# A cross-attention and FFN kernel: the next block's fourth query product moves from ahead of the seventh values to behind the eighth

## The reference, cut to what matters

```python
x = x + _L0_xattn_ref(_layernorm(x), ctx_1024, ctx_1024, Wq, Wk, Wv, Wo, lam, g)
x = x + _L0_ffn_ref(_layernorm(x), ln1_g, ln1_b, w1, b1, ln2_g, ln2_b, w2, b2)

# _L0_xattn_ref: 16 heads of width 32, 8 key/value heads, two softmax maps for each head
w = softmax(q1 @ k1.T) - lam * softmax(q2 @ k2.T)
attn = w @ v
attn = attn * rsqrt(mean(attn * attn) + EPS) * g * (1.0 - LAMBDA_INIT)
return attn @ Wo.T

# _L0_ffn_ref: both weight matrices are rounded to three levels first
h = gelu(layer_norm(x, ln1_g, ln1_b) @ w1q.T + b1)
out = layer_norm(h, ln2_g, ln2_b) @ w2q.T + b2
```

## Time and profile before

| | |
|---|---|
| median of 3 runs | 2423.88 us (2423.76 to 2427.24) |
| the profiled execution | 2423.49 us, of which the span from first to last instruction is 2421.5 us |
| PE busy | 2286.6 us, 94% |
| DVE busy | 1714.2 us, 71% |
| ACT busy | 1339.7 us, 55% |
| GpSimd busy | 993.4 us, 41% |
| mean granted TensorE clock | 0.983 of full speed |

### The profile page before, as it was taken

How to read it: one execution, slowest core, us unless ns; L and a number is a source line. 1 busy time by engine, 2 the same in 40 slices (tenths; PEclk the granted TensorE clock), 3 DMA queues, 4 the chain that set the end, 5 groups by cost and what they waited for, 6 DMA issues and landing times.

```text
span 2421.5 us, 35774 instructions
## 1 busy us (share of the span) xinstructions
PE 2286.6 (94%) x13791; PEld 1083.1 (45%) x13791; DVE 1714.2 (71%) x2701; ACT 1339.7 (55%) x1945; POOL 993.4 (41%) x807
## 2 busy tenths in 40 slices
PE   8679999999999999999989999999999999999978
PEld 5344534445353544535344454534445453544433
DVE  4677768686785868678676867868676786867663
ACT  3435655556465555656555555655556565555544
POOL 0102625436172534627153452715346271534517
PEclk9779999999999999999999999999999999999989
DMA  7412103030210303021130302112040211203000
GB/s 262 120 25 62 27 24 83 15 92 15 78 30 29 78 15 92 15 66 27 43 79 15 92 15 66 28 47 59 15 107 15 66 28 50 56 15 75 15 22 18
DMA packets 105661, 125.88 MB, mean 52 GB/s; under 512 B 22512, under 2 KB 74284, under 8 KB 104980
## 3 DMA queue, kind: packets, MB, share of 16 engines
q1 hardware_dynamic: 105492, 123.60, 18.4%
HBM read 51.80 MB, written 20.36 MB: 30 GB/s over the span
## 4 chain that ended last, share of the span: by engine, by line
PE 70%; DVE 17%; DMA 3%; ACT 3%; POOL 3%; issue 3%; SPq 1%; POOLq 0%; ACTq 0%; DVEq 0%
PE ps L1421 16%; PE ps L1443 9%; PE ps L1433 9%; PE ps L1319 5%; PE ps L1366 5%; PE ps L1344 4%; PE ps L1264 4%; PE ps L1373 4%; PE ps L1265 3%; PE ps L1266 3%; DVE attn_raw L993 2%; DVE arena L1052 2%; DVE arena L941 2%; DMA arena<-in_x 2%; DVE arena L955 2%
## 5 line engine op out<-in xcount | busy, mean ns | idle before, releaser
L563 POOL TENSOR_TENSOR attn_raw<-attn_raw 128x512 f32<-128x512 f32 x448 | 579.1, 1311 | 153.5 <-ACT attn_raw L720 146.2
L1421 PE MATMUL ps<-rows,w1T 128*128 128x512 f16 x2048 | 486.9, 381 | 24.8 <-DVE rows L1047 24.8
L955 DVE TENSOR_REDUCE arena<-ps 128x3 f32<-128x462 f32 (+1 forms) x704 | 413.0, 618 | 111.0 <-PE ps L1319 110.1
L529 POOL TENSOR_TENSOR q<-q 128x512 f16<-128x512 f32 x128 | 158.3, 1241 | 723.3 <-ACT q L666 706.6
L715 ACT ACTIVATE attn_raw<-ps,vec_cols,wstep 128x512 f32<-128x512 f32 x256 | 198.7, 776 | 276.3 <-PE ps L1421 274.4
L1052 DVE SCALAR_TENSOR_TENSOR arena<-attn_raw,vec_cols,arena 128x512 f16<-128x512 f32 x256 | 231.8, 905 | 86.1 <-ACT arena L718 84.5
L1421 PEld LDWEIGHTS ps<-rows,w1T 128*128 128x128 f16 x2048 | 191.8, 98 | 222.1 <-DVE rows L1047 38.0
L1443 PE MATMUL ps<-w2T,arena 128*128 128x512 f16 x1088 | 271.2, 379 | 0.0
L686 ACT ACTIVATE arena<-ps 128x1024 f32<-128x1024 f32 x128 | 131.6, 1028 | 228.3 <-PE ps L1344 228.3
L975 DVE SCALAR_TENSOR_TENSOR p<-arena,p 128x512 f16<-128x512 f32 x128 | 88.1, 688 | 236.7 <-ACT p L690 236.7
L1319 PE MATMUL ps<-k_att,stack_raw 96*128 96x154 f16 x2048 | 222.0, 233 | 27.2 <-DVE arena L955 25.2
(11 more groups left out here) (183 smaller groups left out, 3478.7 us busy)
## 6 DMA issues: line engine op xcount, KB each, us to landing
stack_raw<-q SPq DMA_DIRECT2D x768, 64.0 KB, 2.0
arena<-in_x SPq DMA_DIRECT2D x64, 256.0 KB, 2.7
out<-arena SPq DMA_DIRECT2D x64, 256.0 KB, 2.1
arena<-in_x SPq DMA_DIRECT2D x15, 1024.0 KB, 6.2
arena<-in_L_ffn_w SPq DMA_DIRECT2D x7, 1024.0 KB, 10.1
stack_raw<-in_L_xattn_Wq SPq DMA_DIRECT2D x8, 256.0 KB, 5.8
k_att<-k_store SPq DMA_DIRECT2D x4, 490.0 KB
k_store<-attn_raw SPq DMA_DIRECT2D x12, 160.0 KB
```

The source lines that it names most:

```text
L563: ins = pool.tensor_tensor(acc[:, e, :], acc[:, e, :], src[:, j % NG, :], ALU.add)
L955: dve.tensor_reduce(negmax[:, tt, u0:u1], ps[:, row_bank(c, tb), 0:(u1 - u0) * S].rearrange("p (u s) -> p u s", s=S), AX.X, ALU.max, negat ...
L1421: ins = pe.matmul(ps[:, B_H + j % 2, :], w1T[:, k, j * P:(j + 1) * P], rows16[:, e, k, :], start=(k == 0 and e == 0), stop=(k == KD - 1 an ...
```

## The change

In the string that blocks 1 to 15 walk, the token `q3` moves from between `s7` and `v6` to between `v7` and `a3`. Block 15 skips it, so the order changes in 14 blocks, 1 to 14. No work is added or taken away.

```diff
 ATTEND = [(w[0], int(w[1:] or 0)) for w in (
-    "e2 g f2 y0 y1 s0 q0 z0 z1 y2 s1 v0 s2 h3 v1 s3 i3 v2 y3 s4 a0 v3 s5 q1 z2 v4 s6 a1 q2 v5 z3 s7 q3 v6 a2 v7 a3").split()]
+    "e2 g f2 y0 y1 s0 q0 z0 z1 y2 s1 v0 s2 h3 v1 s3 i3 v2 y3 s4 a0 v3 s5 q1 z2 v4 s6 a1 q2 v5 z3 s7 v6 a2 v7 q3 a3").split()]
```

## The result

The changed kernel takes 2431.44 us (median of 20 runs, 2427.72 to 2435.14) against 2424.78 before (20 runs, 2420.71 to 2428.84): ratio 1.0026, 95% interval 1.0020 to 1.0033. It is 6.7 us slower; 7.8 was forecast. 2431.7 was predicted, with 2428.6 to 2436.8 as the range. That the time falls 0.3 from the forecast is partly luck: the kernel before, too, measured 0.9 more here than the 2423.88 that the forecast started from.

A forecast was written before the change was run, and what follows sets the result against it. TensorE, busy 94% of the span, and its waits were taken to bound the kernel. 9 x 0.81 + 1.36 - 4 x 0.21 = +7.8 us on the median 2423.88 gave 2431.7, range 2428.6 to 2436.8.

The forecast's parts named there:

- Steps 1 and 2: Behind scores(7), values(6) and values(7) start earlier; the rest of values(7) then stalls on VectorE's L975, as block 15 shows, 1.94.
- Step 3: On VectorE's chain to L975, L997 takes 0.69 instead of 0.90 without L529 beside it: 0.21 off, stall 1.96.
- Step 6: Other engines: the product's ACT operations, L529 beside a reciprocal and SP's later stacking of the pair, costed at nothing.
- Step 4: Behind values(7), TensorE reaches pair 3 and rms_sums 1.36 late: the new stall of 1.96 less the 0.59 wait removed.
- Step 5: At L1007 and hidden, VectorE's slack of 0.55 absorbs part of TensorE's delay, so both come 0.81 late.
- The sum over blocks: Over 14 changed blocks: nine pay 0.81, block 14 pays 1.36, four gain 0.21; +7.8 us.
- The count of four late blocks: In blocks 3, 7, 10 and 11, VectorE's wait for late input rows hides TensorE's delay of 0.81.
- the last sign of being wrong: The forecast is wrong if late transfers fall in blocks other than 3, 7, 10 and 11.
- the 0.21 that each of the four was to gain: In blocks 3, 7, 10 and 11, the input rows' transfer is issued 0.21 earlier, behind L1087.
- The rival "faster": At values(7), L975 is done before 1063.1, so no stall: 11.7 us less, 2412.2; chance 0.05.
- rival on the clock: TensorE falls to 1.2 GHz for the output projection after stalls of 1.96 us; over 70 us, above 2490; chance 0.02.

The follow-up runs named there:

- q3_between: The product q3 put between v6 and v7 (s7 v6 q3 a2 v7 a3), compared with the kernel before: 2422.25 us, ratio 0.9991.
- early_after: Changed kernel with z3 (L1087) and group 7's L975 moved ahead of the reciprocal in normalise(5), compared with the kernel before: 2417.85 us, ratio 0.9972.
- half_before: Kernel before with two of the four row tiles of ln1_rows moved behind h_lo on VectorE: 2410.58 us, ratio 0.9940.
- half_after: Changed kernel with two of the four row tiles of ln1_rows moved behind h_lo, compared with the kernel before: 2420.82 us, ratio 0.9985.
- after_again: The changed kernel run once more, unaltered, compared with the kernel before: 2430.25 us, ratio 1.0027.
- z3_before: Kernel before with z3 (L1087) alone moved ahead of the reciprocal of normalise(5), L975 staying behind: 2415.16 us, ratio 0.9968.
- z3_after: Changed kernel with z3 (L1087) alone moved ahead of the reciprocal of normalise(5), compared with the kernel before: 2426.48 us, ratio 1.0009.
- early_before: Kernel before with z3 (L1087) and group 7's L975 moved ahead of the reciprocal in normalise(5): 2414.31 us, ratio 0.9957.
- early_half_after: Changed kernel with z3 and L975 ahead of the reciprocal and half of ln1_rows behind h_lo, compared with the kernel before: 2401.06 us, ratio 0.9903.
- early_after_late_lo: Changed kernel with z3 and L975 ahead of the reciprocal and L529 behind a3's squares, compared with the kernel before: 2407.45 us, ratio 0.9939.
- all_three: Changed kernel with z3 and L975 early, half of ln1_rows behind h_lo, L529 behind a3's squares, against the kernel before: 2392.34 us, ratio 0.9877.

## Why the prediction was right

- *Steps 1 and 2, a new wait for L975.* Right: the bracket of 1.94, 15 times, 29.0 us with block 15's. Shown by taking it away in two ways: q3_between puts the cover back and the loss goes; early_after brings L975 forward and the stall goes, and with L529 out of the way too the new place is ahead.
- *Step 3, L997 shorter once L529 is elsewhere.* Right: 0.69 in all blocks, and in q3_between too. The Trainium skill's rule (SBUF — State Buffer, Who interferes with whom: VectorE operations with two SBUF inputs and GpSimd's reads exclude each other) also holds for the new place. Step 6 had put L529 beside a reciprocal there, with one input, and it is: L529 starts at 1076.43, the reciprocal lasts from 1075.16 to 1078.51 and keeps its 3.35. What no step priced are the squares of `a2`: they now run beside L1001 and take 1.73 instead of 1.27, without harm: no engine waits for them there. The expectation for early_after left out where L529 would fall, and there the same rule cost 0.8 us a block.
- *Step 4, 1.36 late at `rms_sums`.* Measured 1.34. *Step 5, 0.81 late at L1007 and at `hidden`.* Measured 0.78 and 0.81; half_before against half_after shows the slack to be what takes 1.34 down to 0.8.
- *Step 6, costed at nothing.* L1007 and `hidden` are within 0.03 of where steps 4 and 5 put them, so nothing else reached them.
- *The sum over blocks.* 7.8 by the forecast, 6.7 by the medians with an interval of 4.8 to 8.0, and 8.4 between the two profiled spans. The count of four late blocks held: late rows move `hidden` in blocks 3, 7, 10 and 11 before, in 2, 3, 7 and 11 after, and in 3, 7, 10 and 11 of after_again; those of block 12 after and of block 6 in after_again end within L1007's wait for `rms_sums`, and L1007 keeps its 21.97. But the last sign of being wrong came in part: block 10 was late before, block 2 after. And the 0.21 that each of the four was to gain is lost in how long the transfers take: counted from the undisturbed 35.67, late rows put `hidden` back by 10.9 us in all before, by 11.5 after and by 8.7 in after_again, where 10.9 - 0.8 = 10.1 was forecast. The two traces after lie 1.4 to either side of the forecast, so this term is good on average and not for one trace, and the 1.1 us between forecast and median are no more than it can move. z3_before against z3_after shows what the late rows hide: 11.3 us without them.
- *The rest of 8.4.* At `scores(7)` of block 15 the changed kernel is 9.6 behind (2324.88 against 2315.29) and gets 1.2 back behind it. The profiles differ by such amounts there whatever the change: from that point to the end takes 106.25 before, 105.04 after, and 103.6 to 106.5 in the other runs, all with a granted clock that is for a time at 0.50.
- *The rival "faster"* named the right mechanism with a wrong price. It asked for L975 ahead of the reciprocal and promised 11.7 us under the kernel before. L975 alone does not pay that. With it moved, `values(7)` ends near 7.3 behind `scores(7)`, but VectorE has the reciprocal, L1000 and L1004 to do first, all behind the moved steps, and comes to L988 of `normalise(7)` only at 9.68, no earlier than in the changed kernel (1072.57 - 1062.99 = 9.58); and L992 then hangs on GpSimd. With L529 late, pair 3 comes at 17.78, where the rival had it (1074.57 - 1056.83 = 17.74), but L1007 at 20.63 and not at 20.04, for it ends VectorE's own chain through `ln1_stats`. Against the kernel before with the same VectorE moves, the product's new place costs 3.5 us while L529 falls on L992, and gains 6.9 us once L529 comes later.

That late rows come from the transfers of residual rows and keys issued just ahead is not shown by itself, but the rows speak for it. In block 10 the input rows' load is issued 10.29 behind `scores(7)` before and lands 10.0 us later; in z3_before, where the residual rows are loaded some 4 us earlier, it is issued at 10.22 and lands 5.6 us later. In z3_before and early_before it takes 5.5 to 6.6 us in all of blocks 1 to 13. In early_after it is issued at 7.57, close behind the residual rows again, and takes 8.1 to 9.7 us in blocks 3, 4, 6, 7 and 11; it starts early enough there to be in time all the same. In blocks 3, 7 and 11, z3 also lets it be issued 1.0 us earlier (10.22 instead of 11.25).

## What to carry to other kernels

Work that stands in a place where nobody seems to need it may be the cover of a dependency on another engine: before moving it, look in the trace for what ends last if it goes (here the last block, which lacks the work, showed the 1.94 us stall to be expected). Price a delay at the next point where engines meet, and count how many blocks have slack there for another reason. When an engine's step is moved, check what runs beside it on VectorE and GpSimd in the new place as well as in the old.

## What the runs showed of the hardware

A GpSimd operation on 128x512 held up a VectorE operation with two SBUF inputs that began while it ran: 1.55 us instead of 0.75, and 0.90 instead of 0.69. In q3_between L1001 takes 1.22 instead of 0.69:

```profile
1068.17 1.16 POOL L529 TENSOR_TENSOR q<-q 128x512 f16<-128x512 f32 x1 [7.55 <-ACT q L666]
...
1068.65 1.22 DVE L1001 SCALAR_TENSOR_TENSOR rows<-attn_raw,rows 128x512 f16<-128x512 f32 x1 [0.70 <-ACT rows L694]
```

In each of the three the VectorE operation ends 0.54 to 0.55 us behind GpSimd's. It goes the other way too: in the changed kernel the squares of `a2`, which start 0.08 us behind a VectorE operation with two SBUF inputs (L1001, 0.68 long), take 1.73 us instead of 1.27. In the timelines of VectorE and GpSimd:

```profile
1071.09 0.68 DVE L1001 SCALAR_TENSOR_TENSOR rows<-attn_raw,rows 128x512 f16<-128x512 f32 x1
...
1071.17 1.73 POOL L542 TENSOR_TENSOR sq_acc<-sq_acc,attn_raw 128x512 f32<-128x512 f32 x1 [7.33 <-ACT attn_raw L699]
```

A stall of 1.94 us on TensorE in each of 14 blocks, and one of 3.14, left the granted clock of those stretches at 1.00, the 2.4 GHz level. Other idle times were followed by the 1.2 GHz level, some of them only in some executions. In block 7 of q3_between VectorE waited 5.06 us for input rows and TensorE then idled 4.24; the next matmuls start 0.43 apart instead of 0.22:

```profile
1228.17 0.59 PE L1264 MATMUL ps<-arena,wqT_hi 128*128 128x512 f16 x1 [4.24 <-DVE arena L1016]
...
1229.00:1233.00 4.00, 4.00 (x11) 1.46 (x10) 3.88 (x12) 0.00 (x0) 1.82 (x2) 0.50 0.22 50
```

In block 15 of early_after and of early_half_after a stall of 2.14 us, with L1004 as releaser, was followed by some 3 us at 0.50, and pair 3 came 1.5 us later than in early_before, early_after_late_lo and all_three, where the same stall left the clock at 1.00. The rows are of early_after and of early_before, with the clock as the third number from the end:

```profile
2323.16 0.40 PE L1269 MATMUL ps<-woT_hi,rows 128*128 128x512 f16 x1 [2.14 <-DVE rows L1004]
2324.00:2326.00 2.00, 2.00 (x6) 0.69 (x5) 1.96 (x4) 0.00 (x0) 0.24 (x1) 0.50 0.00 0
...
2315.19 0.39 PE L1269 MATMUL ps<-woT_hi,rows 128*128 128x512 f16 x1 [2.14 <-DVE rows L1004]
2316.00:2318.00 2.00, 2.00 (x11) 0.88 (x9) 1.97 (x4) 0.00 (x0) 0.27 (x1) 1.00 0.00 0
```

A wait of 1.70 us at the second scores of block 15 is in both profiles of the changed kernel; behind it the clock is 0.50 for some 3 us in after_again and 1.00 in the first. So the prediction's rival on the clock did not come true in the 14 blocks, but waits no longer than the new one were followed by the slower clock elsewhere, and one profile does not settle such a case. What decides it is not shown.
